# A twelve-stage perceiver on one core: shielded groups in the second cross attention, a new written-out order in three of the four, and frame weights loaded a stage earlier

## The chip, the cores and the metric

One core of a Trainium2 chip. The metric is the device time of one launch in microseconds (us). Matmuls run on TensorE (PE), elementwise work on VectorE (DVE), ScalarE (ACT) and GpSimd (POOL); SyncE (SP) issues most of the loads and stores.

## The reference

A stream x of 256 tokens by 256 channels goes through four layers. Each layer adds three things to x: a cross attention onto 4096 context tokens (16 heads of 16 channels), another mixing stage, and a feed-forward stage. In short:

```
x += cross0(norm(x), ctx, mask, group_prob)   # softmax(q k + (1-mask)*-1e9) * group_prob, times v
x += taylor_attention(norm(x));  x += top1_expert(norm(x))
x += cross1(norm(x), ctx, mask)               # softmax(where(mask == 0, -1e9, q k / 4)) times v
x += frame_attention(norm(norm(x)) * g + b);  x += experts_that_choose_tokens(norm(x))
x += cross2(norm(x), ctx, key_mask);          x += plain_attention; x += zone_experts
x += cross3(norm(x), ctx);                    x += recurrence;      x += gelu_feed_forward
```

The mask of cross0 and cross1 is 256 x 4096 integers, 0 or 1. A query of cross1 whose mask is 0 for every key attends to all keys evenly.

## The kernel before, in words

All keys and values of the four layers are projected first (`project_context`), split into three bf16 parts and stored to DRAM. Each cross attention is then one `attend` stage, which computes every score twice. For head h:

- **Step C** (`by_queries`, L727): one matmul makes 128 queries x 512 keys. DVE takes its row maximum from PSUM (`chunk_max`, L874 with the mask added, or L878 without one). Sixteen C make a head. They go through a ring of three PSUM banks, so a C waits until DVE has read the bank of three C before. C runs 24 chunks (1.5 heads) ahead, 30 in the first attention.
- POOL splits the negated maximum into three bf16 parts (`split`); **step T** (`turn_max`, L792) transposes them; ACT writes them into three rows of the query operand (`place_max`, L845). The next scores thereby come out with the maximum already taken off.
- **Step K** (`by_keys`, L741): four matmuls of 128 keys x 256 queries, one *group* of eight per head. With `by_query` (the first two attentions) one matmul more for each pair, identity times `neg_k`, adds -2^100 for masked keys (L744). ACT takes the exponential of the 128 x 1024 group from PSUM (L861) into one of NP buffers `prob`. Two pairs of banks alternate, so K waits for ACT to have read the group two back.
- **Step V** (`values`, L766): 16 matmuls for two groups, which gather values and denominators in bank 7. In the first attention DVE (L891) and POOL (L973) multiply groups by `gT` before V.
- After a head's last V, ACT reads the sums (`read_sums`, L850); **step F** (`fold`, L801) brings them together in a ring bank, and DVE divides (`normalise`, L899 and L901).

The order on PE comes from nested loops with a period W (2 in the first attention, 4 in the others). Written with these letters, one head is, in the first attention, `CCK KCCV CCKT KCCFV CCK KCCV CCK KCCV`, and in the other three `CCK CCK CCK KCC VV CCK CCKT CCKF KCC VV`. The first VV of a head takes groups 4 to 7 of the head before, the last takes groups 0 to 3 of the same head. The last head and a half have no C, since C runs ahead.

Before each later attention, `queries` fills the time of the norm with matmuls that keep TensorE busy (`keep_warm`, L209), projects the queries, stores and reloads them. After the second attention, `frames` loads its own weights (`m_gb`, three `m_w` of 1 MB, `m_wo` of 1 MB), its bias `m_bo`, the key mask of the third attention (`m_raw`), the first weights of the next stage (`e_router`, `e_w`) and the third attention's keys (`kop`), all from SP's queue and in this order.

Of the kernel before, what the change touches and what calls it, by code (L numbers as in the profile page):

```python
# [24 lines left out]
P = 128  # L25
D = 256
# [14 lines left out]
KEYED = 2  # L41
NORM_FILL, FOLD_FILL, TOP_FILL = 16, 6, 28
# [17 lines left out]
Q_DONE = 16 * len(Q_BESIDE)  # L60

# [519 lines left out]
def fill_constants(c, pool, S):  # L581

    for tile, value in ((c.idle, 0.0), (c.fold, 0.0), (c.ones, 1.0), (c.tri, 0.5), (c.den16, 0.0)):
        pool.memset(tile[:, :], value).then_inc(S("later_filled"), 1)
# [17 lines left out]
def queries(c, l, ctx):  # L602
# [5 lines left out]
    banks = (1, 2)  # L608
    stage = Stage(S)

    @stage.vector
    def _(dve):
        norm_dve(c, dve, S, c.x, c.xn)
        dve.memset(c.qop[96:P, :, :], 0.0).then_inc(S("qop_set"), 1)
        q.rest_and_third(dve, S, banks)

# [5 lines left out]
    def _(pe):  # L622
        keep_warm(c, pe, NORM_FILL)
# [27 lines left out]
def attend(c, l, by_query, weighted, ctx, asked, load_next):  # L651
# [4 lines left out]
    W = 2 if weighted else 4  # L656
    NP = 2 * W
# [28 lines left out]
    own = [g for g in range(NGROUP) if g not in SHARED]  # L686

# [19 lines left out]
    def _(pe):  # L707
# [22 lines left out]
        def by_keys(h, g):  # L730

            n = NGROUP * h + g
            if n < 2:
                pe.wait_ge(S("first_read"), last_first[st_order[n]] + 1)
            else:
# [3 lines left out]
            for j in range(GROUP):  # L739
                k = g * GROUP + j  # L740
                ins = pe.matmul(st_bank(n)[:, j * NT:(j + 1) * NT], kop[0:R_ALL, h % UNROLL, k * P:(k + 1) * P],  # L741
                                qop[0:R_ALL, h, :], start=(j % 2 == 0), stop=(not by_query and j % 2 == 1))
                if by_query and j % 2 == 1:
# [12 lines left out]
        def values(n):  # L756
# [14 lines left out]
        def phase(groups):  # L771

            for n in groups:
# [9 lines left out]
            for n in groups:  # L783
# [32 lines left out]
        for h in range(H):  # L816
            for g in range(NGROUP):
                if g % W == W - 1:
                    by_keys(h, g)
                for i in range(2):  # L820
                    at = SC * h + 2 * g + i + AHEAD
# [4 lines left out]
                if g % W != W - 1:  # L826
                    by_keys(h, g)
                if g == TURN_AT and h + 1 < H:
                    turn_max(h + 1)
                if g == FOLD_AT and h > 0:  # L830
                    fold(h - 1)
                if (g + 1) % W == 0:
                    done = NGROUP * h + g + 1
                    phase(range(max(done - 2 * W, 0), done - W))
        phase(range(NGROUP * H - W, NGROUP * H))
# [1677 lines left out]
```

## Time and profile before

| | |
|---|---|
| median of 3 runs | 1584.65 us (1582.46 to 1588.14) |
| the profiled execution: its time, its span | 1583.62 us, 1582.4 us |
| mean granted TensorE clock | 0.960 of full speed |
| PE, DVE, ACT, POOL busy | 1462.9, 978.0, 717.1, 410.3 us |
| steps K of the second attention begin, its last sums are read | 662.24, 896.96 us |
| steps K of the third attention begin, its last sums are read | 1037.15, 1233.18 us |
| one head of the second, of the third attention | 14.89, 12.31 us |

A matmul of 512 columns shows as 0.38 us but the next one begins about 0.22 us after it, so the time a step takes on PE is read from the starts of consecutive rows. In the same way an ACT exponential of 128 x 1024 shows 1.02 us, and two back to back show 1.94.

### The profile page before, as it was taken

The numbers are of one execution on the slowest core, as the hardware profiler recorded it, in microseconds if no ns is written. First come the engines' busy times: TensorE is split into PE (matmuls) and PEld (weight loads), VectorE is DVE, ScalarE is ACT, GpSimd is POOL, SyncE is SP. The second block draws the span as 40 slices with busy tenths as digits, with TensorE's granted clock in tenths as the row PEclk, the third lists the DMA queues.
The fourth block names the chain that finished last, engine by engine and source line by source line (L and its number), as shares of the span: only waits on it lengthen the run. The fifth ranks groups of instructions, "written<-read, shape, count | busy, mean of one in ns | idle before, by whom it ended". The sixth has DMA issues, their size and how long they took to land. (4 is left out here: it accounts for less than half of the span.)

```text
span 1582.4 us, 29922 instructions
## 1 busy us (share of the span) xinstructions
PE 1462.9 (92%) x11296; PEld 846.9 (54%) x11296; DVE 978.0 (62%) x2273; ACT 717.1 (45%) x972; POOL 410.3 (26%) x584
## 2 busy tenths in 40 slices
PE   8999987999999988799999888799999897999997
PEld 3665753555555556255555455345555583555555
DVE  4443446888888744777777224388886236888832
ACT  5134221444444531265665433256767221767662
POOL 4555332656666620101101022011111001011100
PEclk9999996999999998799999989889999997999999
DMA  8888992334446043264551094536667521566700
GB/s 272 267 277 255 284 298 84 62 61 62 61 65 151 2 72 50 51 88 76 78 88 35 12 293 151 146 56 96 91 103 212 85 36 44 87 95 93 158 3 7
DMA packets 131658, 178.23 MB, mean 113 GB/s; under 512 B 14365, under 2 KB 105525, under 8 KB 124342
## 3 DMA queue, kind: packets, MB, share of 16 engines
q1 hardware_dynamic: 117610, 160.90, 48.1%
q10 hardware_dynamic: 13904, 15.41, 3.1%
q8 instruction: 90, 1.47, 0.4%
q14 instruction: 54, 0.44, 0.1%
HBM read 132.44 MB, written 43.78 MB: 111 GB/s over the span
## 5 line engine op out<-in xcount | busy, mean ns | idle before, releaser
L861 ACT ACTIVATE prob_a<-ps 128x1024 f32<-128x1024 f32 x512 | 505.5, 1023 | 305.2 <-PE ps L744 215.9
L874 DVE CUSTOM_DVE_ANT_0 dump_a<-ps,neg_q 128x512 bf16<-128x512 f32 (+1 forms) x485 | 328.6, 717 | 104.0 <-PE ps L727 102.5
L727 PE MATMUL ps<-kop,qop 116*128 116x512 bf16 x1024 | 347.4, 410 | 41.1 <-DMA qop<-qparts 23.4
L878 DVE TENSOR_REDUCE best_a<-ps 128x1 f32<-128x512 f32 (+1 forms) x488 | 312.6, 707 | 72.4 <-PE ps L727 72.3
L741 PE MATMUL ps<-qop,kop 116*128 116x256 bf16 x2048 | 350.8, 275 | 5.5 <-ACT prob_a L861 4.9
L741 PEld LDWEIGHTS ps<-qop,kop 116*128 116x128 bf16 x2048 | 196.0, 100 | 138.0 <-ACT prob_a L861 17.9
L727 PEld LDWEIGHTS ps<-kop,qop 116*128 116x128 bf16 x1024 | 87.2, 100 | 205.8 <-issue 85.1
L744 PE MATMUL ps<-neg_k,identb 128*128 128x512 bf16 x512 | 195.5, 382 | 0.0
L766 PE MATMUL ps<-prob_a,vop_a 128*32 128x256 f32 x3072 | 185.0, 382 | 0.0
L952 POOL CAST mpart_a<-nmax_a 128x2 bf16<-128x2 f32 x64 | 25.4, 396 | 601.3 <-DVE nmax_a L883 601.3
L973 POOL TENSOR_TENSOR used_a<-prob_a,gT 128x1024 f32<-128x1024 f32 x64 | 151.5, 2367 | 87.5 <-DVE used_a L891 67.4
L766 PEld LDWEIGHTS ps<-prob_a,vop_a 128*32 128x32 f32 x3072 | 90.5, 109 | 82.5 <-issue 26.8
L443 PE MATMUL ps<-wv,ctxT 128*128 128x256 f32 x512 | 114.2, 384 | 10.6 <-DVE vst L542 10.6
L432 PE MATMUL ps<-ctxT,wk 128*128 128x512 f32 x256 | 112.4, 599 | 5.6 <-DMA wk<-in_wk 5.6
L443 PEld LDWEIGHTS ps<-wv,ctxT 128*128 128x128 f32 x512 | 98.0, 192 | 28.0 <-DVE vst L542 12.8
L474 ACT ACTIVATE kp<-ps,bk 128x512 bf16<-128x512 f32 x64 | 43.8, 686 | 123.4 <-PE ps L432 101.9
L891 DVE TENSOR_TENSOR used_a<-prob_a,gT 128x1024 f32<-128x1024 f32 x64 | 94.9, 1482 | 6.5 <-ACT prob_a L861 6.5
L533 DVE SCALAR_TENSOR_TENSOR rest<-ps,bk,kp 128x512 f32<-128x512 f32 x64 | 48.0, 751 | 75.8 <-POOL kp L562 38.2
L562 POOL TENSOR_TENSOR kp<-rest,kp 128x512 bf16<-128x512 f32 x64 | 73.7, 1156 | 66.1 <-ACT kp L479 66.0
L542 DVE TENSOR_TENSOR vst<-ps,bv 128x256 f32<-128x256 f32 x128 | 52.3, 423 | 56.4 <-PE ps L443 42.5
L432 PEld LDWEIGHTS ps<-ctxT,wk 128*128 128x128 f32 x256 | 49.0, 192 | 65.7 <-issue 58.7
L193 POOL TENSOR_TENSOR rstd<-var,minus_half 128x2 f32<-128x2 f32 x11 | 7.8, 713 | 253.2 <-DVE var L183 226.0
(310 smaller groups left out, 1363.1 us busy)
## 6 DMA issues: line engine op xcount, KB each, us to landing
kop<-kparts SPq DMA_DIRECT2D x448, 128.0 KB, 5.1
kparts<-kp SPq DMA_DIRECT2D x64, 384.0 KB, 4.5
vals<-vst SPq DMA_DIRECT2D x16, 1024.0 KB, 6.4
vraw<-vals SPq DMA_DIRECT2D x64, 256.0 KB, 6.4
e_w<-in_e_w SPq DMA_DIRECT2D x6, 2048.0 KB, 16.6
z_w<-in_z_w SPq DMA_DIRECT2D x24, 256.0 KB, 7.2
ctxT<-in_ctxT SPq DMA_DIRECT2D x8, 512.0 KB, 8.1
raw<-in_mask ACTq DMA_DIRECT2D x16, 256.0 KB, 5.8
```

The costliest lines, as they stand in the source:

```text
L432: ins = pe.matmul(c.ps[:, K_BANKS[u % 4], :], wk[:, ct, mt * P:(mt + 1) * P], ctxT[:, ct, j * CHUNK:(j + 1) * CHUNK], start=(ct == 0), sto ...
L443: ins = pe.matmul(c.ps[:, V_BANKS[v % 4], 0:D], ctxT[:, ct, k * P:(k + 1) * P], wv[:, ct, :], start=(ct == 0), stop=(ct == CT - 1))
L562: pool.tensor_tensor(kp[:, u % SLOTS, 2, :], rest[:, u % RESTS, :], kp[:, u % SLOTS, 1, :], ALU.subtract)\
L727: return pe.matmul(out, qop[0:R_ALL, h, t * P:(t + 1) * P], kop[0:R_ALL, h % UNROLL, j * CHUNK:(j + 1) * CHUNK], start=True, stop=True)
L741: ins = pe.matmul(st_bank(n)[:, j * NT:(j + 1) * NT], kop[0:R_ALL, h % UNROLL, k * P:(k + 1) * P], qop[0:R_ALL, h, :], start=(j % 2 == 0), ...
L744: ins = pe.matmul(st_bank(n)[:, (j - 1) * NT:(j + 1) * NT], c.identb[:, :], c.neg_k[:, k - 1:k + 1, :], start=False, stop=True)
L766: ins = pe.matmul(sums_out[32 * j:32 * j + 32, :], vop[:, h % 2, g * GROUP + j, :], used[:, n % NP, j * NT:(j + 1) * NT], start=(g == 0 an ...
L861: act.activation(prob[:, n % NP, :], st_bank(n), ACT.Exp).then_inc(S("exp_done"), 1)
L874: dve.tensor_tensor_reduce(out=dump[:, k % 2, 0:width], in0=bank, in1=c.neg_q[:, t, j * CHUNK:j * CHUNK + width], scale=1.0, scalar=-3.0e3 ...
L878: dve.tensor_reduce(out, bank, AX.X, ALU.max).then_inc(sem, 1)
L891: dve.tensor_tensor(used[:, n % NP, :], prob[:, n % NP, :], c.gT[:, g * GROUP:(g + 1) * GROUP, :].rearrange("p k q -> p (k q)"), ALU.mult)\
L973: pool.tensor_tensor(used[:, n % NP, :], prob[:, n % NP, :], c.gT[:, g * GROUP:(g + 1) * GROUP, :].rearrange("p k q -> p (k q)"), ALU.mult)\
```

## The change

Four parts. No arithmetic of the first attention's steps is altered, and its written order spells what its loops already did.

1. *Shield.* In the second attention, groups 2, 5 and 7 of each head leave out the mask matmuls. ACT computes relu(-score) from PSUM, then exp(-that) in place, so that an unmasked score above the maximum is bounded by 1; POOL then multiplies by a 0/1 mask in bf16, made in place from `neg_k` once (`find_seen`, six POOL instructions of 128 x 1024). V of these groups waits for POOL; K waits only for the relu. Queries with no visible key (`blind`) are found by a sum over `neg_k` on PE, which takes the place of the 16 `keep_warm` matmuls in that one `queries`.
2. *Order.* The steps are written as strings: `MASKED_ORDER` for the second attention and `PLAIN_ORDER` for the third and fourth. One V of the string is two groups. The ACT reading of the sums in the second attention moves from behind group 3 to behind group 2.
3. *Frame weights.* `gT` stays allocated; `m_w` and `m_wo` lie in it and are loaded at the end of the second attention's SP queue. In `frames`, SP now issues `m_bo`, then `e_router` and `e_w`, then the key mask. `w2` of the choosing experts also lies in `gT`.
4. `idle`, the moving operand of `keep_warm`, holds ones instead of zeros.

```diff
+WEIGHTED_ORDER = "CCK KCCV CCKT KCCFV CCK KCCV CCK KCCV".replace(" ", "")
+MASKED_ORDER = "CCK CCK CCK CVV CCK KCCKF CKCT KCCC VV".replace(" ", "")
+PLAIN_ORDER = "CCKCKCCV CCKCKCV CKCCT KF CKCCKC VV".replace(" ", "")
...
-    for tile, value in ((c.idle, 0.0), ...
+    for tile, value in ((c.idle, 1.0), ...
...
+        if l == SHIELDED:                      # queries, vector
+            dve.wait_ge(S("masks_summed"), 1)
+            dve.tensor_scalar(blind[:, :], c.ps[:, 7, 0:NT], (KEYS - 0.5) * NEG, None, ALU.is_le)
...
+        if l == SHIELDED:                      # queries, tensor
+            for k in range(KT):
+                ins = pe.matmul(c.ps[:, 7, 0:NT], c.idle[:, 0:P], c.neg_k[:, k, :], start=(k == 0), stop=(k == KT - 1))
+            ins.then_inc(S("masks_summed"), 1)
+        else:
+            keep_warm(c, pe, NORM_FILL)
...
-    SUM_AT, TURN_AT, FOLD_AT = (W - 1, W, W + 1) if weighted else (W - 1, W + 1, W + 2)
+    ORDER = WEIGHTED_ORDER if weighted else MASKED_ORDER if by_query else PLAIN_ORDER
+    SUM_AT, TURN_AT = (1, 2) if weighted else (2, 5) if by_query else (3, 5)
+    SHIELD = (2, 5, 7) if l == SHIELDED else ()
...
+            elif (n - 2) % NGROUP in SHIELD:   # by_keys
+                pe.wait_ge(S("bounded"), shields(n - 2) + 1)
...
+                added = by_query and g not in SHIELD
-                if by_query and j % 2 == 1:
+                if added and j % 2 == 1:
...
+            elif g in SHIELD:                  # values
+                pe.wait_ge(S("shielded"), shields(n) + 1)
...
+                if g in SHIELD:                # scalar
+                    act.activation(prob[:, n % NP, :], st_bank(n), ACT.Relu, scale=-1.0).then_inc(S("bounded"), 1)
+                    act.wait_ge(S("bounded"), shields(n) + 1)
+                    act.activation(prob[:, n % NP, :], prob[:, n % NP, :], ACT.Exp, scale=-1.0).then_inc(S("exp_done"), 1)
...
+        def find_seen(i, g):                   # gpsimd
+            pool.tensor_scalar(seen(g), seen(g), 0.0, None, ALU.is_equal).then_inc(S("seen_found"), 1)
+            pool.wait_ge(S("seen_found"), 2 * i + 1)
+            pool.tensor_tensor(seen(g), seen(g), asked.blind[:, :].unsqueeze(1).to_broadcast((P, GROUP, NT)), ALU.add)\
+                .then_inc(S("seen_found"), 1)
+        def shield(h, g):
+            n = NGROUP * h + g
+            pool.wait_ge(S("exp_done"), n + 1)
+            if h == 0 and g == SHIELD[0]:
+                pool.wait_ge(S("seen_found"), 2 * len(SHIELD))
+            pool.tensor_tensor(prob[:, n % NP, :], prob[:, n % NP, :], seen(g).rearrange("p k q -> p (k q)"), ALU.mult)\
+                .then_inc(S("shielded"), 1)
...
         fill(0)
+        if l == SHIELDED:
+            pool.wait_ge(asked.S("blind_found"), 1)
+            for i, g in enumerate(SHIELD):
+                find_seen(i, g)
         split(0)
...
         for h in range(H):
+            for g in SHIELD[:1]:
+                shield(h, g)
             if h + 1 < H:
                 split(h + 1)
+            for g in SHIELD[1:2]:
+                shield(h, g)
...
             if not SHARED and 0 < h < H - 1:
                 fill(h + 1)
+            for g in SHIELD[2:]:
+                shield(h, g)
...
         def _(sp):                             # frames, sync
-            sp.dma_start(gb[:, :, :], c.a["m_gb"]).then_inc(S("scales"), 16)
-            for k in range(3):
-                sp.dma_start(w[:, k, :, :], tiles(c.a["m_w"])[:, :, k * INNER:(k + 1) * INNER]).then_inc(S(f"w{k}"), 16)
             sp.dma_start(bo[:, :], c.a["m_bo"].to_broadcast((P, D))).then_inc(S("bias_loaded"), 16)
-            sp.dma_start(wo[:, :, :], tiles(c.a["m_wo"])).then_inc(S("wo"), 16)
+            load_next(sp)
             sp.dma_start(raw8[:, :], c.a["mask_keys"]).then_inc(S("keymask_loaded"), 16)
-            load_next(sp)
...
-            cross(c, 1, True, False)
+                cross(c, 1, True, False, for_frames.load)
```

## Rows read from the trace of the kernel before

**Rows 1.** One head's window: us, PE, PEld, DVE, ACT, POOL busy, clock, DMA share, GB/s
```profile
707.23:722.12 14.89, 14.89 (x135) 8.47 (x134) 11.02 (x36) 8.85 (x11) 1.33 (x5) 1.00 0.55 80
1176.54:1188.85 12.31, 12.12 (x120) 6.54 (x119) 10.19 (x20) 8.61 (x11) 1.33 (x5) 1.00 0.65 97
```

**Rows 2.** Timeline of PE in the second attention (start us, us shown, instruction)
```profile
711.05 1.93 PE L766 MATMUL ps<-prob_a,vop_a 128*32 128x256 f32 x32
712.92 0.61 PE L727 MATMUL ps<-kop,qop 116*128 116x512 bf16 x2
713.36 0.38 PE L741 MATMUL ps<-qop,kop 116*128 116x256 bf16 x2
713.58 0.38 PE L744 MATMUL ps<-neg_k,identb 128*128 128x512 bf16 x1
713.80 0.38 PE L741 MATMUL ps<-qop,kop 116*128 116x256 bf16 x2
```

**Rows 3.** Timeline of PE in a head of the third attention
```profile
1175.68 0.39 PE L727 MATMUL ps<-kop,qop 116*128 116x512 bf16 x1 [0.15 <-DVE best_a L878]
...
1182.29 0.56 PE L801 MATMUL ps<-fold,acc_a 128*128 128x32 f32 x4
1182.69 0.60 PE L741 MATMUL ps<-qop,kop 116*128 116x256 bf16 x4
```

**Rows 4.** Timeline of DVE in the same head
```profile
1173.73 4.87 DVE L878 TENSOR_REDUCE best_a<-ps 128x1 f32<-128x512 f32 x8 [1.17 <-PE ps L727]
...
1179.69 3.68 DVE L878 TENSOR_REDUCE best_a<-ps 128x1 f32<-128x512 f32 x6 [0.88 <-PE ps L727]
```

**Rows 5.** First attention, 272 to 560 us: POOL's and DVE's products, DVE's masked maximum
```profile
L973 POOL TENSOR_TENSOR used_a<-prob_a,gT x63: 2350/2367/2379, 273.1 to 558.0; 128x1024 f32<-128x1024 f32 x63
L891 DVE TENSOR_TENSOR used_a<-prob_a,gT x63: 1217/1220/3308, 275.0 to 558.9; 128x1024 f32<-128x1024 f32 x63
L874 DVE CUSTOM_DVE_ANT_0 dump_a<-ps,neg_q x224: 676/685/692, 272.6 to 533.0; 128x512 bf16<-128x512 f32 x112
```

**Rows 6.** Groups by form: work like that which the change adds
```profile
L562 POOL TENSOR_TENSOR kp<-rest,kp 128x512 bf16<-128x512 f32 x64 | 73.7, 1156 | 66.1 <-ACT kp L479 66.0
L479 ACT ACTIVATE kp<-rest 128x512 bf16<-128x512 f32 x64 | 39.8, 621 | 3.3 <-DVE rest L533 3.3
```

**Rows 7.** Timeline of ACT at the end of the second attention
```profile
893.34 1.02 ACT L861 ACTIVATE prob_a<-ps 128x1024 f32<-128x1024 f32 x1 [0.22 <-PE ps L744]
896.96 0.38 ACT L850 ACTIVATE acc_a<-ps 128x256 f32<-128x256 f32 x1 [2.60 <-PE ps L766]
```

**Rows 8.** Start of the second attention: DVE, then POOL
```profile
642.23 0.43 DVE L307 TENSOR_TENSOR qp_q<-qrest_q,qp_q 128x256 bf16<-128x256 f32 x1
...
658.77 0.19 POOL L952 CAST mpart_a<-nmax_a 128x2 bf16<-128x2 f32 x1 [20.94 <-DVE nmax_a L883]
```

**Rows 9.** Timelines at the start of the frame attention: PE and ACT
```profile
907.20 0.60 PE L200 MATMUL ps<-ident,att 128*128 128x128 f32 x4
912.16 12.83 PE L1053 MATMUL ps<-xT,m_w 128*128 128x256 f32 x48 [4.37 <-DMA m_w<-in_m_w]
...
915.95 0.60 ACT L1535 ACTIVATE m_qT<-ps 128x512 f32<-128x512 f32 x1 [6.78 <-PE ps L1053]
```

**Rows 10.** The same stage: POOL and SP's issues
```profile
922.07 3.60 POOL L1435 TENSOR_SCALAR m_neg_row<-m_raw 1x4096 bf16<-1x4096 uint8 x1 [2.00 <-DMA m_raw<-in_mask_keys]
935.52 1.64 POOL L1443 TENSOR_SCALAR m_pn<-m_p,m_rden 128x128 f32<-128x128 f32 x4 [9.86 <-DVE m_rden L1594]
...
909.69 4.46 SPq L1417 DMA_DIRECT2D m_raw<-in_mask_keys  x1
914.62 6.07 SPq L1724 DMA_DIRECT2D e_w<-in_e_w  x2
```

**Rows 11.** The recurrence's first projection on PE; the exponential's table loads on ACT
```profile
1549.16 3.72 PE L1053 MATMUL ps<-xT,r_w 128*128 128x256 f32 x16 [1.11 <-ACT xT L2245]
...
L631 ACT ACT_TABLE_LOAD  x2: 1283/1283/1283, 1007.9 to 1312.4; - x2
```

More of the change, by code:

```diff
@@ L581, in fill_constants @@
 def fill_constants(c, pool, S):
-    for tile, value in ((c.idle, 0.0), (c.fold, 0.0), (c.ones, 1.0), (c.tri, 0.5), (c.den16, 0.0)):
+    for tile, value in ((c.idle, 1.0), (c.fold, 0.0), (c.ones, 1.0), (c.tri, 0.5), (c.den16, 0.0)):
         pool.memset(tile[:, :], value).then_inc(S("later_filled"), 1)
@@ L769, in values, with two_values @@
             ins.then_inc(S("pv_psum"), 1)
-        def phase(groups):
-            for n in groups:
+        def two_values(first):
+            for n in (first, first + 1):
                 if n % NGROUP == 0:
@@ L782, in phase @@
                     sums(n)
-            for n in groups:
+            for n in (first, first + 1):
                 values(n)
@@ L816, in _ @@
         for h in range(H):
[L817 to L821, printed above, removed]
+            at, g, n = SC * h + AHEAD, 0, NGROUP * h - LAG
+            for step in ORDER:
+                if step == "C":
                     if at < SC * H:
@@ L825, in _ @@
                         by_queries(ring_bank(), at).then_inc(S("s_psum"), 1)
-                if g % W != W - 1:
+                    at += 1
+                elif step == "K":
                     by_keys(h, g)
-                if g == TURN_AT and h + 1 < H:
+                    g += 1
+                elif step == "V":
+                    if n >= 0:
+                        two_values(n)
+                    n += 2
+                elif step == "T" and h + 1 < H:
                     turn_max(h + 1)
-                if g == FOLD_AT and h > 0:
+                elif step == "F" and h > 0:
                     fold(h - 1)
[L832 to L835, printed above, removed]
+        for n in range(NGROUP * H - LAG, NGROUP * H, 2):
+            two_values(n)
         fold(H - 1)
@@ L918, in _ @@
         for h in range(H):
-            for g in range(NGROUP):
-                for i in range(2):
-                    at = SC * h + 2 * g + i + AHEAD
+            at = SC * h + AHEAD
+            for step in ORDER:
+                if step == "C":
                     if at < SC * H:
@@ L932, in _ @@
                             row_max(at // SC)
-                n = NGROUP * h + g - 1
-                if weighted and n >= 0 and n % NGROUP in own:
-                    weigh(n)
-                if g == FOLD_AT and h > 0:
+                    at += 1
+                    n = NGROUP * h + (at - AHEAD - SC * h) // 2 - 2
+                    if weighted and (at - AHEAD) % 2 == 0 and n >= 0 and n % NGROUP in own:
+                        weigh(n)
+                elif step == "F" and h > 0:
                     normalise(h - 1)
@@ L1372, in add_bias_pool, with __init__, load, frames @@
         .then_inc(S("bias_added"), 1)
-def frames(c, load_next):
+class FrameWeights:
+    HIDDEN = 1024
+    def __init__(self, c, ctx):
+        self.c = c
+        self.S = Sems(c.nc, ctx, "frames_w")
+        n = 3 * CT * self.HIDDEN // NT
+        self.w = c.gT[:, 0:n, :].rearrange("p (k t m) n -> p k t (m n)", k=3, t=CT)
+        self.wo = c.gT[:, n:n + self.HIDDEN // P, :]
+        self.gb = ctx.enter_context(c.nc.sbuf_tensor("m_gb", [P, 2, CT], F32))
+    def load(self, sp):
+        a = self.c.a
+        sp.dma_start(self.gb[:, :, :], a["m_gb"]).then_inc(self.S("scales"), 16)
+        for k in range(3):
+            sp.dma_start(self.w[:, k, :, :], tiles(a["m_w"])[:, :, k * self.HIDDEN:(k + 1) * self.HIDDEN])\
+              .then_inc(self.S(f"w{k}"), 16)
+        sp.dma_start(self.wo, tiles(a["m_wo"])).then_inc(self.S("wo"), 16)
+def frames(c, weights, load_next):
     nc = c.nc
```

73 lines of the change are left out of this document (40 added, 33 removed).

## The prediction

> **What bounds the kernel now.** I read the page first. It has PE busy for 92% of the span, but a busy PE on it is not PE at its peak, so I went on to windows of one head, then to the timelines of PE, DVE and ACT inside them, and last to the waits at the borders of stages.
>
> One head of the second attention takes 14.89 us [rows 1]. From the starts of consecutive rows, two C cost 0.44 us, two matmuls of K 0.22, a mask matmul 0.22 and four groups of V 1.87 [rows 2]; a fold costs 0.40 [rows 3]. So C is 8 x 0.44 = 3.5, K 16 x 0.22 = 3.5, the mask 16 x 0.22 = 3.5, V 2 x 1.87 = 3.74, F 0.40, T about 0.11 (256 columns, half of a K pair's): 14.8. Nothing is left over: PE itself is the bound there, and DVE (11.02), ACT (8.85) and POOL (1.33) have room [rows 1].
>
> One head of the third attention has the same list without the mask, 11.25 us, and takes 12.31 [rows 1]. The other 1.06 us is waiting, although the window shows PE busy for 12.12: C waits for DVE to free a ring bank [rows 3], and DVE in turn stands dry for 1.17 and 0.88 us behind the two VV of a head [rows 4]. A maximum costs DVE 4.87 / 8 = 0.60 us, three banks hold less than 1.87 us of them, so each VV starves DVE, and PE pays afterwards, when DVE cannot make up what it lost. DVE needs 10.19 us of a head, near PE's 11.25, so neither has the slack to absorb 2 us. The fourth attention has the same program.
>
> **Part 1, the shield.** It takes away 2 mask matmuls in 3 groups, 6 x 0.22 = 1.31 us of PE per head. PE would need 14.89 - 1.31 = 13.58. What it adds must fit under that.
>
> *ACT.* Three relu from PSUM, three exponentials from SBUF. The relu is not in the trace; I take the exponential's 1.02 of the same shape from PSUM [rows 7]. For the exponential from SBUF the nearest row is a copy of half the size at 621 ns [rows 6]: twice that, 1.24, is the upper bound, the lower is 0.92 (the pace of two exponentials back to back in 1.94). I take 1.05 with its wait. ACT has 8.85 of work [rows 1], plus 3 x 1.02, so 11.9; even with the upper bounds 12.5, under 13.58.
>
> *POOL.* The product of 128 x 1024 takes 2.37 [rows 5]; that row has f32 for both operands, and one with a bf16 operand of half the size takes 1.16 [rows 6], so 2.31 to 2.37. Three are 7.1 and with the old 1.33 make 8.4.
>
> *The chain within a head.* I laid one head of MASKED_ORDER on PE with these prices, from its first C at 0. K0 ends 1.3, K1 2.6, K2 (short, 0.44) 3.5, VV 5.6, K3 6.9, K4 7.8, K5 (short) 8.7, F 9.0, K6 10.1, T 10.3, K7 10.9, the last VV runs 11.6 to 13.5. ACT behind it: exp0 2.5, exp1 3.8, relu2 4.8, exp2 5.9, the sums 6.3 (its place behind group 2, after the first VV), exp3 8.1, exp4 9.0, relu5 10.1, exp5 11.1, the turned maximum 11.5, exp6 12.5, relu7 13.5, exp7 14.6. K waits only for the reading two groups back: K5 begins 8.2 and needs exp3 (8.1), K6 9.2 and needs exp4 (9.0), K7 10.4 and needs relu5 (10.1). These are the tightest three, 0.1 to 0.3 us each, and a release takes about 0.15 of that, so small stalls of up to 0.1 are possible; each would let the next one slip. POOL: group 2 from 5.9 to 8.4, the split to 9.4 (T wants it at 10.2), group 5 from 11.2 to 13.6, the fill of values 14.2, group 7 to 17.1, which is 3.5 in the next head, where V of groups 6 and 7 begins 4.7. All hidden, the narrowest by 0.8 for T. Under the old order K would wait, since a third group's two ACT steps fall against K3; that is why the order matters here.
>
> *Start.* The sum over the mask has the 8192 columns of the 16 filling matmuls that it replaces: 0. `blind` is ready at about 643.1 (one more small DVE step after 642.66 [rows 8]). Six POOL steps of at most 2.31 give 13.9 us at most, to 657.0; the first split would have begun at 658.77. Cover 1.8 us at least: 0. If it were gone, each us late delays T, hence the first K, one for one.
>
> *End.* C is absent from the last head, which PE now does in 14.89 - 3.5 = 11.4. After the change PE could take 10.1, but ACT needs 12.0: instead of a gain a loss of 0.6. Behind the last K, the row shows exponential, then 2.60 us until the sums [rows 7]; now relu, exponential, POOL's 2.37 and V of one group: 1.7 us later.
>
> Sum: 14.5 heads x 1.31 = 19.0, less 0.6, less 1.7: **-16.7**; with stalls of 0.1 per head at K5 to K7, -15. I take -16. Ends: -19 (no loss at the end) and -7 (0.6 us stalls in each head).
>
> On DVE against POOL: while POOL multiplies through the first attention, DVE's masked maximum keeps 676 to 692 ns over 224 executions, but DVE's own product of two SBUF operands goes from 1217 up to 3308 [rows 5]. The Trainium skill (SBUF — State Buffer, "SBUF: two separate sides") says the pair of ports is held for a whole instruction against a DVE step with two SBUF inputs; the maximum has one, its other input being PSUM, so by that rule, and by the row, it is free.
>
> **Part 2, the order.** In the second attention it is counted above. In the third and fourth, PLAIN_ORDER has two single V (0.94 each) and one VV in place of two VV. A single V with the next C (0.22) and its release (0.2) keeps DVE without new work for about 1.35 us, against up to 1.2 buffered: dry by 0.15 at most. One VV remains: dry about 1.1. So DVE's head is 10.2 + 1.1 + 0.2 = 11.5, PE's 11.25, and the head goes from 12.31 to about **11.5**. T now stands one K earlier; its three maximum parts come 8 C into the head plus about 1.2 us of POOL, which leaves a stall of 0.1 to 0.2 now and then, inside that 11.5. The last head and a half are ACT's and stay. 13.5 x 0.8 = 10.9 each: **-22** for both. Ends: PE's floor 11.25, 13.5 x 1.06 = 14.3 each, -29; and no gain, 0.
>
> **Part 3, frame weights.** PE ends its transposes at 907.8 and could project once ACT has scaled; the same shape of step in the recurrence has PE idle for 1.11 us [rows 11]. Here 4.37, until `m_w` [rows 9]: -3.0 (I keep 0.2 for the row's ends). The first project then took 915.95 - 912.16 = 3.8 us with the clock low after the gap, where the recurrence runs 16 matmuls in 3.72 with its short gap [rows 9, 11], so 8 in 1.8: another -1.9, if the clock holds. Sum **-4.7**, ends -2.8 and -5. SP: the five issues move to the second attention's queue, behind its last `kop` load, four heads before the end of C's keys, some 50 us: 0. In `frames` the key mask moves behind `e_w`: POOL needs it 3.60 us ahead of its first `m_pn`, at 935.52, now 930.8 [rows 10]. Only `m_bo` now stands before `e_w`, so `e_w` is begun by 909.7 at the latest; with its 6.07 and the mask's 4.46 the mask is issued by 920.2. In the old place it landed at 922.1, 7.9 us after its issue ended. With 7.9 again it would be there at 928.1 and POOL ready at 931.7, 0.9 us late. But 6.07, 4.46 and 7.9 were all measured behind 4 MB of `m_w` and `m_wo`, which are gone from the queue, so I take 0. If POOL is late, it takes back 0.9 to 4.
>
> **Part 4 and the first attention.** Ones for zeros in the filling matmuls: same shapes, 0. The first attention's string spells its loops: 0.
>
> **Sum.** -16 - 22 - 4.7 = -43 against the profiled execution's 1583.6: 1541. The median of the runs is 1 us above it: **1541.5**.
>
> **Rivals.**
> - *A. PE is already full in the third and fourth attention.* The window's 12.12 of 12.31 speaks for it; the waits of C and DVE's dry stretches against it. Then part 2 gives 0 to -6: 1584.65 - 16 - 4.7 - 3 = 1561.
> - *B. ACT's chain stalls K in the second attention*, from 0.1 to 0.3 us of room: at 0.6 us a head, part 1 gives -7: 1551.
> - *C. The relu reloads ACT's table.* A load is 1283 ns [rows 11]; two switches per shielded group are 6 x 1.28 = 7.7 us per head, ACT 11.9 + 7.7 = 19.6 against PE's 13.6: +4.7 a head instead of -1.3, +75: 1584.65 + 75 - 27 = 1633. It decides from 2 switches a head on, and nothing in the trace excludes it, since no relu runs there; copies between exponentials reload nothing. The Trainium skill (ScalarE: Activation LUTs, "Table sets: the hidden batching unit") puts relu in every set: by that rule C does not occur.
> - *D. POOL blocks DVE's maxima.* 7.1 us more for DVE per head: 11.02 + 7.1 = 18.1, +3.2 a head: about 1608. [rows 5] speak against it.
> - *E. The change does more*: PE's floor everywhere, 1584.65 - 19 - 29 - 5 = 1532.
>
> **Chances.** Forecast (1534 to 1549) 0.62; A 0.13; B 0.13; E 0.06; C 0.03; D 0.01; the key mask's cover lost (1546) 0.02. The measurement tells 0.3%, 5 us, from nothing. Range 1531 to 1558: it holds the forecast, E, B and the milder half of A. Faster 0.95, same 0.01 (A and B together, with frame gains lost), slower 0.04 (C, D).
>
> **What would show it.** Right: heads of 13.5 to 13.7 us in the second attention without ACT ahead of K in PE's waits, 11.4 to 11.6 in the other two with DVE dry once a head, PE's first `m_w` matmul about 1.3 us behind the transposes with its first eight in 1.8. Wrong: PE waits for the relu or POOL in V; table loads among the exponentials; heads of the third attention still near 12.3; POOL's first `m_pn` waiting for the key mask.

## The result, and the profile after

The changed kernel takes **1542.33 us** (median of 4 runs, 1537.95 to 1543.41) against 1585.02 (4 runs, 1582.46 to 1588.14): a ratio of 0.9725, 95% interval 0.9699 to 0.9751. I had predicted 1541.5, with 1531 to 1558 as the range. The profiled execution of the changed kernel took 1537.95 us, the lowest of its runs; its span is 1536.7, that of before 1582.4. The two profiles thus differ by 45.7 us and the medians by 42.7.

Where the 45.7 went I read from ACT's timeline, between two instructions that every attention has: the first eviction of a turned maximum (`qop`) and the last of an accumulator (`acc_a`).

| stretch | before | after | difference |
|---|---|---|---|
| start to the first attention | 264.01 | 264.49 | +0.5 |
| first attention | 301.96 | 301.89 | -0.1 |
| to the second | 94.36 | 94.52 | +0.2 |
| second attention | 236.63 | 219.80 | **-16.8** |
| to the third (frame attention in it) | 138.37 | 130.33 | **-8.0** |
| third attention | 197.85 | 187.30 | **-10.6** |
| to the fourth | 106.25 | 106.02 | -0.2 |
| fourth attention | 197.77 | 187.21 | **-10.6** |
| to the end | 45.2 | 45.14 | -0.1 |

The windows of one head in the second and in the third attention (us, then PE, PEld, DVE, ACT, POOL busy, clock, DMA share, GB/s), which answer to [rows 1]:

```profile
708.44:722.01 13.57, 13.57 (x129) 7.88 (x128) 10.89 (x35) 11.64 (x14) 7.68 (x8) 1.00 0.59 89
1129.62:1141.27 11.65, 11.65 (x122) 6.73 (x119) 10.34 (x19) 8.55 (x10) 1.32 (x5) 1.00 0.70 103
```

PE is full in both, where it had 0.19 us of visible gaps in the third attention. ACT has gained 2.8 us a head in the second, POOL 6.35, and both still fit. The groups of the second attention, 661 to 880 us, by form (busy us, mean ns | idle before), show the new work and the DVE step that it could have blocked:

```profile
L894 ACT ACTIVATE prob_a<-ps 128x1024 f32<-128x1024 f32 x80 | 80.1, 1023 | 29.2 <-PE ps L768 28.8
L892 ACT ACTIVATE prob_a<-prob_a 128x1024 f32<-128x1024 f32 x48 | 50.8, 1057 | 1.5
L890 ACT ACTIVATE prob_a<-ps 128x1024 f32<-128x1024 f32 x48 | 49.1, 1023 | 0.0
...
L1026 POOL TENSOR_TENSOR prob_a<-prob_a,neg_k 128x1024 f32<-128x1024 f32 x48 | 102.4, 2134 | 91.9 <-ACT prob_a L892 86.3 <-issue 5.6
...
L907 DVE CUSTOM_DVE_ANT_0 dump_a<-ps,neg_q 128x512 bf16<-128x512 f32 x232 | 151.9, 689 | 36.7 <-PE ps L748 34.7
```

The relu (L890) lasts exactly as long as an exponential from PSUM, 1.02; the exponential from SBUF 1.06; the product 2.13, below the 2.31 to 2.37 of my bracket. ACT loads no table in the attention. The masked maximum keeps its 689 ns, the same mean as in that stage of before, with POOL now busy for over half of every head.

The third attention, PE's timeline over one head (start us, us shown, instruction), beside [rows 3]:

```profile
1131.71 1.07 PE L792 MATMUL ps<-prob_a,vop_a 128*32 128x256 f32 x16
1132.72 0.61 PE L748 MATMUL ps<-kop,qop 116*128 116x512 bf16 x2
...
1134.25 0.38 PE L748 MATMUL ps<-kop,qop 116*128 116x512 bf16 x1
1134.56 1.07 PE L792 MATMUL ps<-prob_a,vop_a 128*32 128x256 f32 x16
1135.56 0.39 PE L748 MATMUL ps<-kop,qop 116*128 116x512 bf16 x1
...
1139.10 0.38 PE L748 MATMUL ps<-kop,qop 116*128 116x512 bf16 x1
1139.41 1.93 PE L792 MATMUL ps<-prob_a,vop_a 128*32 128x256 f32 x32
1141.27 0.60 PE L748 MATMUL ps<-kop,qop 116*128 116x512 bf16 x2
```

and DVE's in the same stage, beside [rows 4]:

```profile
1124.33 1.94 DVE L911 TENSOR_REDUCE best_a<-ps 128x1 f32<-128x512 f32 x3 [0.15 <-PE ps L748]
...
1130.05 4.98 DVE L911 TENSOR_REDUCE best_a<-ps 128x1 f32<-128x512 f32 x8 [1.08 <-PE ps L748]
```

DVE stands dry for 1.23 us a head instead of 2.05, and no wait is left on PE. Note the distances of the starts on PE: a matmul of C is 0.22 us when another C or a K follows, but 0.31 when V follows (1134.25 to 1134.56), and a single V takes 1.00 to the next C, not half of a VV's 1.86.

The start of the frame attention, PE and ACT, then POOL, beside [rows 9, 10]:

```profile
890.93 0.60 PE L208 MATMUL ps<-ident,att 128*128 128x128 f32 x4
892.64 5.66 PE L1115 MATMUL ps<-xT,gT 128*128 128x256 f32 x25 [1.11 <-ACT xT L1425]
```
```profile
894.67 0.60 ACT L1612 ACTIVATE m_qT<-ps 128x512 f32<-128x512 f32 x1 [2.08 <-PE ps L1115]
```
```profile
906.36 3.59 POOL L1512 TENSOR_SCALAR m_neg_row<-m_raw 1x4096 bf16<-1x4096 uint8 x1 [11.10 <-DMA m_raw<-in_mask_keys]
913.79 1.63 POOL L1520 TENSOR_SCALAR m_pn<-m_p,m_rden 128x128 f32<-128x128 f32 x4 [3.84 <-DVE m_rden L1671]
```

PE waits 1.11 for ACT instead of 4.37 for the weights, and its first eight matmuls take 2.03 (892.64 to 894.67) instead of 3.79. The key mask is done at 909.95, 3.8 us before the first `m_pn`, which waits for DVE. Windows show the clock in both places, first in the kernel after:

```profile
892.64:894.67 2.03, 2.03 (x9) 1.82 (x10) 0.00 (x0) 0.00 (x0) 0.68 (x1) 1.00 0.48 83
...
921.00:926.00 5.00, 4.75 (x44) 3.29 (x44) 2.49 (x12) 3.01 (x13) 2.21 (x6) 1.00 1.01 169
```

and in the kernel before:

```profile
912.16:915.95 3.79, 3.79 (x9) 3.07 (x10) 0.00 (x0) 0.00 (x0) 0.00 (x0) 0.50 1.03 422
944.00:949.00 5.00, 5.00 (x36) 3.32 (x34) 2.35 (x12) 1.81 (x9) 1.10 (x3) 0.66 1.05 202
```

### The profile page after: what moved, and what is told of

Read it like the earlier page. It is cut to its first block and busy times, and to the rows that moved or that the text cites. A ratio compares the mean times of both kernels' runs of the same rounds, so it can differ in the third digit from the quotient of the medians.

```text
span 1536.7 us, 29870 instructions
## 1 busy us (share of the span) xinstructions
PE 1420.2 (92%) x11216; PEld 838.7 (55%) x11216; DVE 980.9 (64%) x2274; ACT 760.1 (49%) x1020; POOL 526.1 (34%) x638
## 5 line engine op out<-in xcount | busy, mean ns | idle before, releaser
L894 ACT ACTIVATE prob_a<-ps 128x1024 f32<-128x1024 f32 x464 | 456.2, 1023 | 268.1 <-PE ps L768 170.7
L748 PE MATMUL ps<-kop,qop 116*128 116x512 bf16 x1024 | 343.8, 405 | 38.0 <-DMA qop<-qparts 22.7
L911 DVE TENSOR_REDUCE best_a<-ps 128x1 f32<-128x512 f32 (+1 forms) x488 | 318.6, 709 | 48.5 <-PE ps L748 48.0
L765 PE MATMUL ps<-qop,kop 116*128 116x256 bf16 x2048 | 343.8, 274 | 3.2 <-ACT prob_a L894 2.6
L792 PE MATMUL ps<-prob_a,vop_a 128*32 128x256 f32 x3072 | 191.7, 383 | 3.1 <-POOL prob_a L1026 2.2
L768 PE MATMUL ps<-neg_k,identb 128*128 128x512 bf16 x416 | 159.0, 382 | 0.0
L1026 POOL TENSOR_TENSOR prob_a<-prob_a,neg_k 128x1024 f32<-128x1024 f32 x48 | 102.4, 2134 | 91.9 <-ACT prob_a L892 86.3
L792 PEld LDWEIGHTS ps<-prob_a,vop_a 128*32 128x32 f32 x3072 | 87.2, 109 | 82.6 <-issue 33.5
## 6 DMA issues: line engine op xcount, KB each, us to landing
e_w<-in_e_w SPq DMA_DIRECT2D x4, 2048.0 KB, 11.4
```

The source lines that it names most:

```text
L748: return pe.matmul(out, qop[0:R_ALL, h, t * P:(t + 1) * P], kop[0:R_ALL, h % UNROLL, j * CHUNK:(j + 1) * CHUNK], start=True, stop=True)
L768: ins = pe.matmul(st_bank(n)[:, (j - 1) * NT:(j + 1) * NT], c.identb[:, :], c.neg_k[:, k - 1:k + 1, :], start=False, stop=True)
L792: ins = pe.matmul(sums_out[32 * j:32 * j + 32, :], vop[:, h % 2, g * GROUP + j, :], used[:, n % NP, j * NT:(j + 1) * NT], start=(g == 0 an ...
L894: act.activation(prob[:, n % NP, :], st_bank(n), ACT.Exp).then_inc(S("exp_done"), 1)
L911: dve.tensor_reduce(out, bank, AX.X, ALU.max).then_inc(sem, 1)
L1026: pool.tensor_tensor(prob[:, n % NP, :], prob[:, n % NP, :], seen(g).rearrange("p k q -> p (k q)"), ALU.mult)\
```

## The experiments

Twelve runs: the changed kernel once more, and eleven kernels made from it. The first four undo one part each. Ratios are to the kernel before in the same set; the changed kernel itself stands at 0.9725.

**The old order in the second attention.**

```diff
-MASKED_ORDER = "CCK CCK CCK CVV CCK KCCKF CKCT KCCC VV"
+MASKED_ORDER = "CCK CCK CCK KCC VV CCK CCKT CCKF KCC VV"
...
-    SUM_AT, TURN_AT = (1, 2) if weighted else (2, 5) if by_query else (3, 5)
+    SUM_AT, TURN_AT = (1, 2) if weighted else (3, 5)
```

> The second attention keeps its three shielded groups but goes back to the order before (CCK CCK CCK KCC VV CCK CCKT CCKF KCC VV, sums read behind group 3). Theory 1 (the new order is needed to collect what the shield frees): three shielded groups meet the old order badly, K3 waits about 0.4 us for ACT and T about 0.1 in each head, so a head takes 14.0 us instead of the 13.57 of the changed kernel, and the whole is 6 to 9 us slower than the changed kernel, about 1550 us, ratio to before near 0.978. Rival (ACT has enough room in any order, the mask matmuls alone set the gain): a head takes 13.6 us and the time is that of the changed kernel, 1542 us, 0.973.

1552.96 us (1548.52 to 1554.22), 0.9805 [0.9789, 0.9821]. Heads of 14.09 and a second attention of 228.5, 8.7 longer than with the new order. PE's timeline shows one wait in a head, at K3, and ACT's shows what it waits for:

```profile
707.40 0.60 PE L765 MATMUL ps<-qop,kop 116*128 116x256 bf16 x4
708.24 0.39 PE L765 MATMUL ps<-qop,kop 116*128 116x256 bf16 x2 [0.24 <-ACT prob_a L894]
```
```profile
707.16 1.02 ACT L894 ACTIVATE prob_a<-ps 128x1024 f32<-128x1024 f32 x1 [0.28 <-PE ps L768]
708.08 1.02 ACT L890 ACTIVATE prob_a<-ps 128x1024 f32<-128x1024 f32 x1
```

K3 begins 0.84 us after K2, which needs only 0.44 without its mask matmuls: 0.40 of the 0.52 that a head loses. What it waits for is the plain exponential of group 1, for which ACT itself had stood idle; the relu of group 2 begins only behind it.

The time is 10.6 above the changed kernel's, where I had expected 6 to 9. So the shield alone, without its order, is worth only 8.1 of the 16.8.

**No shield, new order.**

```diff
-    SHIELD = (2, 5, 7) if l == SHIELDED else ()
+    SHIELD = ()
```

> No group is shielded (all eight add the mask on TensorE again), everything else as in the changed kernel, its new order of the second attention too. Theory 1 (the second attention was PE-bound, so order alone buys nothing there and the 16.8 us come from the six mask matmuls): a head takes 14.8 to 14.9 us, the whole is 16 to 17 us slower than the changed kernel, 1559 us, ratio 0.983. Rival (part of the gain of the second attention comes from the order): a head under 14.6 us and less than 12 us lost, 1554 us or less.

1554.25 us (1553.68 to 1556.34), 0.9814 [0.9797, 0.983]. Heads of 14.89, attention 236.23. The new order buys 0.4 us by itself; the two together buy 16.8. Half of that needs the order. I had expected 1559, and the median is 4.7 below that, where the rival had put it (1554 or less). The two profiled executions differ by 16.2, almost all of it in the second attention; the medians differ by 11.9, since the changed kernel's profiled execution is the fastest of its four. The length of the heads and of the attention decides here, not the medians.

**The old order in the third and fourth attention.**

```diff
-PLAIN_ORDER = "CCKCKCCV CCKCKCV CKCCT KF CKCCKC VV"
+PLAIN_ORDER = "CCK CCK CCK KCC VV CCK CCKT CCKF KCC VV"
```

> Only the third and fourth attention go back to the order before; shield, masked order and early frame weights stay. Theory 1 (two double V per head starve DVE, one does so less): heads of the third attention take 12.31 us again instead of 11.65, each of the two attentions loses 10.5 us, together 21, about 1563 us, ratio 0.986. Rival (the heads got shorter for another reason, such as where tiles lie or what else runs): heads stay at 11.7 us and the time at 1542.

1563.89 us (1559.77 to 1566.15), 0.9868 [0.9847, 0.9888]. Both attentions 198.06, heads of 12.31, and DVE's two dry stretches are back:

```profile
1141.79 4.88 DVE L911 TENSOR_REDUCE best_a<-ps 128x1 f32<-128x512 f32 x8 [1.17 <-PE ps L748]
...
1147.75 3.68 DVE L911 TENSOR_REDUCE best_a<-ps 128x1 f32<-128x512 f32 x6 [0.88 <-PE ps L748]
```

**The frame weights loaded in the frame attention again.**

```diff
+            weights.load(sp)                   # frames, sync
             sp.dma_start(bo[:, :], ...).then_inc(S("bias_loaded"), 16)
-            load_next(sp)
             sp.dma_start(raw8[:, :], c.a["mask_keys"]).then_inc(S("keymask_loaded"), 16)
+            load_next(sp)
...
-                cross(c, 1, True, False, for_frames.load)
+                cross(c, 1, True, False)
```

> The frame weights keep their place in the long-lived tile but are loaded at the start of the frame stage, in the order of the kernel before. Theory 1 (the whole 7.0 us that the frame stage gained comes from this load: 3.3 of waiting, 1.8 of the first projection at half clock, 0.4 of the next, and 1.6 of a later stretch at half clock that goes away with it): the stage takes 74.5 us from the last sums to the stream's addition instead of 67.5, the whole 1549 us. Rival (the later stretch at half clock has nothing to do with the load): only 5.4 us come back, the stretch around the fourth pair of heads stays at full clock.

1549.91 us (1546.44 to 1550.35), 0.9776 [0.976, 0.9792]: 7.6 above the changed kernel. PE waits again, and the slow stretch behind the frame softmax is back too (the stretch from `m_p` to the sum into `x` 41.44 us, as 41.43 before and 39.87 after). From the last sums to the sum into `x` it takes 77.05 us, where I had expected 74.5 and the changed kernel has 67.48:

```profile
882.24 1.08 PE L792 MATMUL ps<-prob_a,vop_a 128*32 128x256 f32 x8 [1.82 <-POOL prob_a L1026]
883.91 1.03 PE L827 MATMUL ps<-fold,acc_a 128*128 128x32 f32 x4 [0.59 <-ACT acc_a L878]
...
900.93 9.35 PE L1115 MATMUL ps<-xT,gT 128*128 128x256 f32 x31 [4.60 <-DMA gT<-in_m_w]
```

Its first two rows show a thing that I had not foreseen: a V and a fold that take 0.64 and 0.60 in the profile of the changed kernel take 1.08 and 1.03 here. The clock falls at the very end of the second attention (granted 0.74 from 880 to 884 us, 0.50 from 884 to 888), and that is most of the 2.5 us more. Two kernels of the next set look at that.

**The changed kernel once more**, as the measure for that set.

> The changed kernel once more, unaltered, beside the others of this set. Theory (the end of the second attention leaves TensorE sparse, and in some executions the granted clock falls right behind it): median 1540 to 1543, runs spread over 1538 to 1544, and the profile shows either 13.97 us from the last accumulator of the second attention to the first query projection of the frame attention (clock 1.00) or 15.6 to 16.8 (clock near 0.5 for some 3 us in it). Rival (only noise): no such stretch, and 13.97 in it.

1542.13 us (5 runs, 1538.28 to 1548.46), 0.9724 [0.9702, 0.9746]. Two of the five lie at 1548, above the 1544 that I had expected as the highest. The profiled execution was one of them, 1548.46, and its PE timeline shows the fall (granted clock 0.68 from 884 to 888 us, 0.50 from 888 to 892):

```profile
885.75 1.08 PE L792 MATMUL ps<-prob_a,vop_a 128*32 128x256 f32 x8 [1.82 <-POOL prob_a L1026]
887.43 1.03 PE L827 MATMUL ps<-fold,acc_a 128*128 128x32 f32 x4 [0.59 <-ACT acc_a L878]
888.27 2.75 PE L217 MATMUL ps<-idle,identb 128*128 128x512 bf16 x6
```

From the last accumulator to the first query projection it takes 16.09 us, 13.97 in the other profile. But of the 10.5 us between the two spans only 2.1 lie there: 3.6 lie ahead of the first attention, 0.9 in it, 1.2 behind it, 0.6 in the second, 1.6 behind the frame softmax, where the clock is 0.68 from 930 to 935 us.

**The last head unshielded.** `seen` gets a tile of its own, and the last head adds its masks on PE in all groups.

```diff
+    shielded = lambda n: n % NGROUP in SHIELD and n // NGROUP < H - 1
+    seen_t = sb("seen", [P, len(SHIELD) * GROUP, NT], BF16) if SHIELD else None
...
-                added = by_query and g not in SHIELD
+                added = by_query and not shielded(n)
```

> The last head of the second attention goes without the shield: its mask is added on TensorE again (6 mask matmuls, 1.31 us more), and behind the last exponential stands no GpSimd product. Theory (the shield costs 0.6 + 1.7 us in the last head, since ACT and GpSimd end it): second attention 217.5 instead of 219.8 us, the wait of 1.83 us for GpSimd is gone; and TensorE stays denser, so 13.97 us in front of the first query projection in every execution: median 2 to 4 us under the changed kernel. Rival (the last head is bound by ACT's evictions either way): second attention 219.5 to 220, median the same.

The profiled execution was disturbed from start to end (4570.4 us, the filling matmuls at a mean of 957 ns) and gives no rows; the five others took 1536.73 to 1545.41, median 1541.22, ratio 0.9717 [0.9699, 0.9735]: not told apart from the changed kernel, and not the 2 to 4 us less that I had expected. The head itself is looked at again below.

**Filling matmuls at the end of the second attention.**

```diff
+            if l == SHIELDED:
+                pe.wait_ge(S("s_read"), slots.n - RING + 1)
+                keep_warm(c, pe, 4, slots.n % RING)
```

> The changed kernel with four idle filling matmuls ahead of each of the last two value groups of the second attention, which keep TensorE busy while ACT and GpSimd end it. Theory (the sparse end lets the clock fall in some executions): second attention unchanged at 219.8, granted clock 1.00 through the stretch, 13.97 us in front of the first query projection, median 0.5 to 2 us lower than the changed kernel's. Rival (no clock effect of that stretch): median the same, within 0.5 us. If the fillers sit in the way: second attention up to 1.8 us longer.

1541.12 us (4 runs, 1538.05 to 1542.17), 0.9711 [0.9697, 0.9726]. The second attention is 219.84 and the stretch behind it 13.98, as expected, but the time isn't told apart from the changed kernel's.

**All value groups single in the third and fourth attention.**

```diff
-PLAIN_ORDER = "CCKCKCCV CCKCKCV CKCCT KF CKCCKC VV"
+PLAIN_ORDER = "CCKCKCV CCKCKCV CKCCKFTK CCV CKCCV"
...
-    SUM_AT, TURN_AT = (1, 2) if weighted else (2, 5) if by_query else (3, 5)
+    SUM_AT, TURN_AT = (1, 2) if weighted else (2, 5) if by_query else (3, 4)
```

> In the third and fourth attention the last pair of value groups is taken apart as well: no two value groups in a row, the turned maximum one group earlier. Theory (each pair starves DVE for about 1.1 us and nothing else holds the head over TensorE's 11.25): the head goes from 11.65 to 11.25 or 11.35, each of the two attentions 4 to 6 us shorter, span 8 to 12 us shorter, time about 1530. Rival (DVE's maxima or ACT pace the head at 11.65 whatever the order): heads of 11.6 to 11.7, time the same, about 1542. The new place of the turned maximum may add a wait for its transposes: then heads of 11.8 and more.

1547.41 us (1543.62 to 1550.46), 0.975 [0.9731, 0.9769]: slower than the changed kernel, and both of my numbers were wrong. The heads are 11.87, the attentions 189.24. PE waits for nothing:

```profile
1094.28 1.07 PE L792 MATMUL ps<-prob_a,vop_a 128*32 128x256 f32 x16
1095.29 0.60 PE L748 MATMUL ps<-kop,qop 116*128 116x512 bf16 x2
...
1096.82 0.38 PE L748 MATMUL ps<-kop,qop 116*128 116x512 bf16 x1
1097.12 1.07 PE L792 MATMUL ps<-prob_a,vop_a 128*32 128x256 f32 x16
```

This told me to add up PE's starts again: 16 C 3.52, 8 K 3.5, four V at 1.00, four entries at 0.09, F 0.37, T 0.12, in all 11.87. The changed kernel by the same prices: 3.52 + 3.5 + 2 x 1.00 + 1.87 + entries of 0.09, 0.09 and 0.12 + 0.37 + 0.12 = 11.68, measured 11.65. A head in single V has more fixed cost on PE, and that, not DVE, is what it pays.

**A little more work for DVE.** Two reciprocals a head in the third and fourth attention, whose results nobody uses.

```diff
+            if not (weighted or by_query):
+                for k in range(2):
+                    dve.reciprocal(spare[:, k, :], folded[:, :, HD])
```

> In the third and fourth attention DVE takes two more reciprocals a head, 0.16 us each, whose result nobody uses: 0.33 us more DVE work per head. Theory (in the new order PE's own list fills the head: 11.25 us of matmuls and 0.4 of fixed time at the entries to and exits from the value groups, and DVE's dry 1.23 us is a consequence): heads stay at 11.65 to 11.7, DVE dry for 0.9, time the same, 1541 to 1543. Rival, my prediction's account (DVE paces the head: its work plus its dry time behind a pair of value groups): heads of 11.95 to 12.0, both attentions 4 to 4.5 us longer, time about 1550.

1539.77 us (1538.97 to 1541.19), 0.9711 [0.9693, 0.973]. The dose was smaller than I had reckoned: the two take 0.23 back to back, and DVE's busy time in a head rises by 0.13 (10.34 to 10.47). The head stays at 11.65, both attentions at 187.3, and the dry stretch shrinks by just that:

```profile
1094.47 0.23 DVE L935 RECIPROCAL spare_a<-ps 128x2 f32<-128x2 f32 x2
...
1098.33 4.98 DVE L912 TENSOR_REDUCE best_a<-ps 128x1 f32<-128x512 f32 x8 [0.95 <-PE ps L749]
```

Had DVE paced the head, 14 heads would have grown by 0.13, the attention by 1.8. The dose is small; but PE also waits for nothing in the head, and its own list adds up to it. PE paces it.

**Zeros in the filling matmuls.** The one part that I had costed at nothing without a row that shows it.

```diff
-    for tile, value in ((c.idle, 1.0), ...
+    for tile, value in ((c.idle, 0.0), (c.full, 1.0), ...
```

> The changed kernel with its filling matmuls multiplying zeros again, as before the change; the ones for the sum over the mask stand in a tile of their own. Nothing else differs. The changed kernel's runs spread over 1538 to 1548, the kernel before's over 3 us in the same set, and the half-clock stretches behind that spread lie also in the first 268 us, where no step was changed but what the filling matmuls multiply. Theory (matmuls of ones bring the half-clock stretches): runs within 4 us, median 1537 to 1539, the first attention begins at 264 to 264.5 in the profile. Rival (the value has no part in it, and the spread is chance): median 1541 to 1543 and the same spread of 8 to 10 us.

1541.96 us (5 runs, 1538.14 to 1547.67), 0.9742 [0.9722, 0.9762]. Median and spread are the changed kernel's. The kernel before spreads as well over the 11 runs of this set, 1582.62 to 1589.55. The theory that ones bring the slow stretches falls; the value costs nothing that shows.

**Zeros, and the last head unshielded.**

> Zeros in the filling matmuls and the last head of the second attention without the shield, both in one kernel. Theory (the shield in the last head costs 0.6 + 1.7 us): second attention 217.5 us in the profile instead of 219.8, no wait for GpSimd at its end, and the median about 2 us below the kernel with zeros alone: 1535 to 1537. Rival (the last head is bound by ACT's evictions with or without the shield): second attention 219.5 to 220, the same time as with zeros alone.

1541.92 us (1536.02 to 1548.12), 0.9734 [0.9708, 0.976]. In the profile the second attention is 218.66, between the two expectations: the wait for POOL is gone. The last two heads take 21.52 instead of 22.95, so 1.4 us is won there, not 2.3 (the first head is 0.3 longer here, as it is with zeros alone). The time is not told apart from the others, and isn't the 1535 to 1537 that I had expected.

**A fourth shielded group.**

```diff
-    SHIELD = (2, 5, 7) if l == SHIELDED else ()
+    SHIELD = (0, 2, 5, 7) if l == SHIELDED else ()
```

> Group 0 is shielded too, four of eight. PE would need 13.57 - 0.44 = 13.13 us a head, ACT 11.9 + 1.0 = 12.9, so a head is 13.15 to 13.25 if the room holds, 5 to 6 us less over the second attention. Finding the unmasked places takes GpSimd 8 steps, 19.6 us instead of 14.8, which makes the first split 4 to 5 us late and the first head longer by that. Theory: second attention 218 to 220 us, no gain to speak of, median within 2 us of the changed kernel. Rival (ACT's steps stall the keys, since group 0 stands beside group 7 of the head before and both are shielded): heads of 13.6 and more, second attention 223 and more.

1543.42 us (1541.11 to 1545.8), 0.9741 [0.9722, 0.976]: no gain. The heads are 13.23 and the second attention 214.72, 5.1 shorter, with ACT at 12.52 of 13.23. Ahead of the attention 3.5 of them are given back: POOL's search for the unmasked places ends so late that the first split waits for it, with no idle time in front:

```profile
659.85 2.12 POOL L1017 TENSOR_TENSOR neg_k<-neg_k,blind_q 128x1024 bf16<-128x1024 bf16 x1
661.92 0.19 POOL L986 CAST mpart_a<-nmax_a 128x2 bf16<-128x2 f32 x1
```

so the stretch from the first attention to the second is 98.01 instead of 94.52. That leaves 1.6 us, less than the medians can tell. In this profile the stretch behind the attention is long too: up to the frame attention's first query it is 19.38 instead of 13.97, with the clock at 0.50 from 880 to 892 us:

```profile
880.00:884.00 4.00, 3.31 (x11) 1.61 (x9) 0.18 (x1) 0.60 (x1) 0.00 (x0) 0.50 0.00 0
884.00:888.00 4.00, 3.63 (x8) 2.37 (x8) 0.33 (x1) 0.00 (x0) 0.00 (x0) 0.50 0.00 0
```

Five other profiles of kernels with three shielded groups have a long stretch there as well (15.60 to 21.34), so it isn't shown to be a price of the fourth group.

No kernel tried beats the changed one by more than its measurement can tell.

## Why the prediction was right, by its own steps

**Part 1, the shield: -16 predicted, -16.8 measured.** The head: 14.89 - 1.31 = 13.58 predicted, 13.57 measured, and no stall at K5 to K7, so ACT's room of 0.1 to 0.3 us held and rival B didn't come. With the old order K does wait, at K3 as I had said and 0.5 us a head in all, but not for my reason ("a third group's two ACT steps fall against K3"): it waits for a plain exponential, because the group without its masks brings PE to K3 too early. Rival C did not come: 48 relu stand between 128 exponentials, and among them no table is loaded. The Trainium skill (ScalarE: Activation LUTs, "Table sets: the hidden batching unit") has relu in every table set, and the trace agrees. Nor did rival D: 689 ns before and after, over 232 maxima with 102 us of POOL's products beside them. The Trainium skill (SBUF — State Buffer, "SBUF: two separate sides") lets GpSimd block a DVE step with two SBUF inputs, which the maximum is not, and the trace agrees here too.

The head's term is right; of the terms at the ends I had left one out, what the order does there by itself. The accumulators' times, in three kernels, take the two apart:

| second attention | before | new order, no shield | changed |
|---|---|---|---|
| to the first accumulator | 22.95 | 21.29 | 20.40 |
| the next thirteen heads | 193.53 | 193.57 | 176.45 |
| the last two heads | 20.15 | 21.37 | 22.95 |

The order wins 1.7 us at the first accumulator and loses 1.2 in the last two heads. The shield wins 0.9 and 17.1, where I had 14.5 heads' worth (19.0), and loses 1.6, where I had 0.6 and 1.7. So the shield is worth 16.4 on top of the order, and the -16.8 is that and the order's 0.4. My gain was 1.0 too high and my loss 0.7 too high, which cancels in part, and the 0.7 that I had allowed for stalls of K did not occur. The kernel with an unshielded last head won back 1.4 of the 1.6.

**At the start** of that attention my cover was thinner than I had claimed. One of the two kinds of POOL step, the comparison in place, takes longer than the bound that I had called the highest:

```profile
643.47 2.80 POOL L1015 TENSOR_SCALAR neg_k<-neg_k 128x1024 bf16<-128x1024 bf16 x1 [5.25 <-DVE blind_q L628]
646.35 2.11 POOL L1017 TENSOR_TENSOR neg_k<-neg_k,blind_q 128x1024 bf16<-128x1024 bf16 x1
...
659.35 0.19 POOL L986 CAST mpart_a<-nmax_a 128x2 bf16<-128x2 f32 x1 [1.02 <-DVE nmax_a L916]
```

The six steps took 14.9 us, not 13.9, and left a cover of 1.0 where I had claimed 1.8 at least. Three groups fit in front of the first split, and a fourth (4.9 us) does not.

**Part 2, the order: -22 predicted, -21.1 measured.** Here the total is near, partly by luck, and the step behind it was wrong: *"So DVE's head is 10.2 + 1.1 + 0.2 = 11.5, PE's 11.25, and the head goes from 12.31 to about 11.5."* The dry times were right (1.08 and 0.15). But PE's 11.25 left out the fixed 0.09 to 0.12 at each entry to V and 0.06 at the exit of each single one, which stand in the distances between PE's starts. With them PE needs 11.65, just outside the 11.4 to 11.6 that I had named as the sign of being right, and is the bound; DVE's dry time no longer costs anything, as the kernel with more DVE work shows. By the same prices (an estimate from the rows above) the old order's own list is 11.43, with two entries to V and no single one: so the new order took away 0.88 us of waiting a head and put 0.22 of transitions in its place. A head thus won 0.66, not 0.8, which over 13.5 heads is 8.9 and not 10.9. The 10.6 was reached because the first accumulator came 1.2 us sooner (19.80 for 21.02) and the last two heads took 0.8 less (16.10 for 16.86), two places that I had put at little or nothing. Leaving out the transitions also made the end "-29, PE's floor" (rival E) unreachable in this order. Rival A is refuted for the kernel before: the old order brings back 12.31 and the dry stretches with it.

**Part 3, the frame weights: -4.7 predicted, -7.0 in the profiles.** The wait fell by 4.37 - 1.11 = 3.26 (predicted 3.0), the projection by 3.79 - 2.03 = 1.76 (predicted 1.9): -5.0. Another 0.45 lies in the rest of the projections, and 1.56 came from a place that I had not looked at, the heads' transposes and values behind the frame softmax, where the clock was 0.66 before and is 1.00 after. With the late weights that stretch is slow again (41.44 us), but it is so in the second profile of the changed kernel too (41.44) and with zeros and the last head unshielded (41.34), and fast in the eight others made from it (39.87 or 39.88), so this 1.6 comes and goes from execution to execution and isn't a firm part of the gain. The key mask was in time by 3.8 us; its transfer isn't slow once the weights are out of its queue, as assumed. The other 1.0 of the 8.0 lies between the frame attention and the third attention and is within what that stretch varies by (62.77 to 63.86 in all profiles).

**The sum.** The second, third and fourth attention and the frame stage make 46.0 (from the unrounded times); the rest of the table adds 0.3, which gives the 45.7 of the profiles. My 43 hit the medians' 42.7 partly by luck: the profiled execution of before lay 1.4 below its median, that of after 4.4 below.

**What stays open.** In the second attention's last head PE is idle for 1.83 us behind POOL. In six of the nine profiles with that end the clock then drops to half and the stretch to the first query projection takes 15.6 to 21.3 us (3.5 of the 21.3 being the wait for weights that were put back); in the other three it takes 13.97 or 13.98. In the three profiles where that end is denser (no shield, last head unshielded, filling matmuls) it is 13.97 or 13.98 each time. At a chance of one in three that would happen once in 27, so it points to the idle time, but the medians of these kernels do not show it, and other stretches scatter as much. That the idle time is the cause is not shown. Nor was it looked into why the new order without the shield takes 1.2 us more for the last two heads.

## What to carry to other kernels

When an engine seems to have room, add up its own list from the distances between starts, transitions included, before calling another engine the bound: here 0.4 us of an 11.65 us head were entries and exits, and the attempt to help DVE further added more of them and won nothing. Taking work off the full engine pays in full only if the order of steps gives the engine that inherits it its time: shield alone 8.1, order alone 0.4, both 16.8. And a stage's preparation must be counted against its cover: a fourth shielded group won 5.1 us inside the attention and lost 3.5 of them ahead of it.

## What the runs showed of the hardware

On GpSimd a comparison with a constant, bf16 to bf16 and in place, took 2.77 to 2.80 us for 128x1024, longer than the sum of two bf16 tensors of that size (2.11). The product of an f32 tensor by a bf16 one took 2.13, that of two f32 tensors 2.37.

On TensorE a matmul of 128x512 in bf16 that is followed by an f32 matmul with 32 weight columns took 0.08 to 0.12 us more to the next start, in the second attention before, in both kinds of attention of the changed kernel and in the order of single value groups (in the old order with the shield, one of a head's two such places took 0.19, and why was not looked into); after sixteen of the latter the next bf16 matmul started 0.06 late, after thirty-two not.

The granted clock fell to its lower level (1.2 GHz) in places that differ between executions of one kernel; in the execution of the changed kernel that took 1548.46 us it is 0.96 over 40 to 80, 160 to 200 and 200 to 240 us, where the one that took 1537.95 has 1.00 in all three, and the first attention begins 3.6 us later. What makes it fall there was not found; with zeros in the filling matmuls the runs spread as widely.
